# Attention maxima in pairs of 512 keys, with the turned maxima kept in the score ring

## The reference

```python
v = (values @ Wv.T).reshape(N, -1, H, Dh)
k = (keys @ Wk.T).reshape(N, -1, H, Dh)
q = (query @ Wq.T).reshape(N, -1, H, Dh)
energy = jnp.einsum('nqhd,nkhd->nhqk', q, k)
attn = jax.nn.softmax(energy / jnp.sqrt(jnp.float32(EMBED_DIM)), axis=3)
out = jnp.einsum('nhql,nlhd->nqhd', attn, v).reshape(N, -1, H * Dh)
return out @ Wo.T + bo
```

## Time and profile before

| what | value |
|---|---|
| timed runs, median of 3 | 3645.14 us (3643.07 to 3645.18) |
| the profiled execution, its own time | 3645.8 us |
| its span, first to last instruction | 3644.0 us |
| granted TensorE clock, mean of the span | 0.966 |
| busy: TensorE matmul, VectorE, ScalarE, GpSimd | 3391.9, 2494.9, 1520.4, 226.7 us |
| attention units, first scores to last values | 316.0 to 1509.4 us |

### The profile page before, as it was taken

The page is one execution under the profiler, slowest core; times in us unless marked ns, Lnnn a source line. Parts: engine busy times, 40 slices in busy tenths (PEclk is TensorE's granted clock), DMA queues, the critical chain, the costliest instruction groups (busy, mean ns, idle before and its releaser), DMA issues. The chain is left out here.

```text
span 3644.0 us, 63094 instructions
## 1 busy us (share of the span) xinstructions
PE 3391.9 (93%) x21900; PEld 2020.3 (55%) x21900; DVE 2494.9 (68%) x5808; ACT 1520.4 (42%) x2718; POOL 226.7 (6%) x251
## 2 busy tenths in 40 slices
PE   8979999999999999769977999977999999999999
PEld 5643222222222222258854545546989898989888
DVE  4538888888888888250013444438888888888885
ACT  4534777777777777412211222212222222222221
POOL 0021100000000000030000000000000000000000
PEclk9987999999999999879988999998999999999999
DMA  5687646465554642141120212112000000000000
GB/s 213 240 253 94 82 64 84 67 78 73 74 78 67 85 63 33 52 174 38 37 86 30 90 59 71 60 55 103 9 13 10 12 10 12 10 12 10 12 10 9
DMA packets 144167, 239.79 MB, mean 66 GB/s; under 512 B 22808, under 2 KB 100224, under 8 KB 143488
## 3 DMA queue, kind: packets, MB, share of 16 engines
q1 hardware_dynamic: 134768, 220.67, 28.6%
q0 software_dynamic: 4608, 12.59, 1.1%
q10 hardware_dynamic: 4624, 4.46, 0.4%
HBM read 170.38 MB, written 66.86 MB: 65 GB/s over the span
## 5 line engine op out<-in xcount | busy, mean ns | idle before, releaser
L656 DVE TENSOR_REDUCE at_pmax<-at_psm 128x2 f32<-128x800 f32 (+1 forms) x1024 | 968.1, 986 | 115.8 <-PE at_psm L504 94.0
L597 ACT ACTIVATE ring<-at_pss 128x512 f32<-128x512 f32 (+1 forms) x1664 | 865.2, 600 | 302.6 <-PE at_pss L518 298.3
L518 PE MATMUL at_pss<-at_qs,at_ks 99*128 99x512 bf16 (+1 forms) x1664 | 506.8, 386 | 8.0 <-ACT ring L597 6.5
L1659 PE MATMUL mt_psd<-mt_xl,mt_key_in 128*128 128x128 f32 x4096 | 491.1, 278 | 2.3 <-DMA mt_key_out<-m_out 2.3
L1659 PEld LDWEIGHTS mt_psd<-mt_xl,mt_key_in 128*128 128x128 f32 x4096 | 469.7, 193 | 3.7 <-DMA mt_key_out<-m_out 2.4
L1685 PE MATMUL mt_psu<-mt_key_out,mt_g 128*128 128x256 f32 x2048 | 447.4, 379 | 1.3 <-DVE mt_g L1895 1.3
L526 PE MATMUL at_pso<-ring,at_vw 128*32 128x512 f32 (+1 forms) x3328 | 444.1, 606 | 0.0
L1685 PEld LDWEIGHTS mt_psu<-mt_key_out,mt_g 128*128 128x128 f32 x2048 | 386.7, 190 | 52.6 <-DVE mt_g L1895 1.4
L502 PE MATMUL at_psm<-at_ks,at_qs 64*128 64x400 bf16 (+1 forms) x1024 | 340.1, 347 | 42.6 <-DVE at_pmax L656 18.9
L502 PEld LDWEIGHTS at_psm<-at_ks,at_qs 64*128 64x128 bf16 x1024 | 88.8, 93 | 467.0 <-DVE at_pmax L656 312.7
L504 PE MATMUL at_psm<-at_kh,at_qh 64*128 64x400 bf16 (+1 forms) x1024 | 339.8, 347 | 0.0
(11 more groups left out here) (218 smaller groups left out, 3781.7 us busy)
## 6 DMA issues: line engine op xcount, KB each, us to landing
at_ks<-k_dram SPq DMA_DIRECT2D x192, 200.1 KB, 6.7
k_dram<-pj_kp SPq DMA_DIRECT2D x24, 800.5 KB, 5.5
v_dram<-pj_v SPq DMA_DIRECT2D x8, 1664.0 KB, 9.1
at_vd<-v_dram SPq DMA_DIRECT2D x32, 416.0 KB, 10.7
pj_ctx<-ctxT SPq DMA_DIRECT2D x8, 1601.0 KB, 11.7
at_kh<-k_dram SPq DMA_DIRECT2D x128, 100.1 KB, 5.6
aw_ctxT<-ctxT SPq DMA_DIRECT2D x8, 1601.0 KB, 7.2
at_qs<-q_dram SPq DMA_DIRECT2D x192, 64.0 KB, 7.0
```

Of the source, the lines that this page charges most:

```text
L518: nc.tensor.matmul(ps_s[0:r, (NST * g + n) % SBANKS, :], ks[:, g, j, kt * P:kt * P + r], qs[:, g, j, :], start=True, stop=True).then_inc(s ...
L597: nc.scalar.activation(pr[0:r, (NST * g + n) % PRING, :], ps_s[0:r, (NST * g + n) % SBANKS, :], ACT.Exp, scale=SCALE).then_inc(expd, 1)
L656: nc.vector.tensor_reduce(pmax[:, 2 * p:2 * p + 2, q, c:c + 1], ps_m[:, n % MBANKS, :, 0:MSPANS[c][1]], AX.X, ALU.max).then_inc(m_red, 1)
L1659: ins = nc.tensor.matmul(ps_d[:, j % 2, y * P:y * P + P], key_in[:, k, j * YB + y, :], xl[:, s, k, :], start=k == 0, stop=k == KC - 1)
```

## The change

The spans become three of 512 keys, the width of one buffer half, and a rest of 65 keys. A unit has 24 jobs with one pair each, and two jobs (one for each head pair) that hold the rest for all four query tiles: eight matmuls of 65 columns, reduced by one instruction with eight results. So there are 26 jobs, two in each step, all between the third and the fourth score; `THREE` and `plan` go.

The turned maxima are written to a slot of the score ring, behind the first score of step 10, and every later score of the ring moves on by one slot. ScalarE copies the turned block to SBUF (`turned_out`) behind the exponential of that score. The split is made by GpSimd out of that copy. The pieces of `invert` move to jobs 14, 16 and 18. The loops of VectorE and GpSimd over the units are written out. The DMA of the bias goes ahead of the first `rows_out`, and before the first unit the six key products that are left stand together.

```diff
...
-    MSPANS = [(a, n) for a, n in spans(KEYS - 1, 400)]
-    MSPANS = [(0, 401)] + [(a + 1, n) for a, n in MSPANS[1:]]
-    NM = len(MSPANS)
-    max_jobs = [(p, q, c) for p in range(HG // 2) for q in range(QT) for c in range(NM)]
+    MSPAN = 512
+    NFULL, REST = KEYS // MSPAN, KEYS % MSPAN
+    NM = NFULL + 1
+    max_jobs = [(p, q, c) for p in range(HG // 2) for q in range(QT) for c in range(NFULL)]
+    max_jobs += [(p, None, NFULL) for p in range(HG // 2)]
...
-    INVERT_IN, INVERT_AT = 3, (17, 18, 22)
+    INVERT_IN, INVERT_AT = 3, (14, 16, 18)
...
-    THREE = (2, 3, 5, 7, 8, 11, 13)
...
-    def pairs_at(kt):
-        return {BETWEEN: 1 if kt == TURN_AT else 2, "values": int(kt in THREE)}
-    EARLY = sum(sum(pairs_at(kt).values()) for kt in range(TURN_AT, KT + 1))
-    order = iter([*range(EARLY, NJ), *range(EARLY)])
-    plan = {kt: {place: [next(order) for _ in range(n)] for place, n in pairs_at(kt).items()} for kt in range(1, KT + 1)}
-    assert next(order, None) is None
+    PER_STEP = NJ // KT
+    assert NJ == PER_STEP * KT and QT * REST <= MSPAN
+    EARLY = PER_STEP * (KT + 1 - TURN_AT)
+    TURN_BEHIND = TURN_AT * HG
+    def jobs_at(kt):
+        first = (kt - 1) * PER_STEP + EARLY
+        return [n % NJ for n in range(first, first + PER_STEP)]
+    def score_slot(u, n):
+        return (1 + u * (NST + 1) + n + (n > TURN_BEHIND)) % SBANKS
+    def turn_slot(u):
+        return ((u - 1) * (NST + 1) + TURN_BEHIND + 2) % SBANKS if u else 0
     with Stage(nc, "at") as st:
...
+        mfull, mrest, mpart = st.sb("mfull", [HG * QT, P]), st.sb("mrest", [HG * QT, P]), st.sb("mpart", [HG * QT, 3, P], BF16)
...
+        bo_in, biased, m_copied, own_split = sem("at_bo"), sem("at_biased"), sem("at_max_copied"), sem("at_own_split")
...
-        turned_at = ps_m[0:HG * QT, 1, 0, 0:P]
+        def turned_at(u):
+            return ps_s[0:HG * QT, turn_slot(u), 0:P]
...
                 for g in range(G - 1):
...
+                sp.dma_start(bo[:, :], t["bo_in"]).then_inc(bo_in, 16)
...
-                sp.dma_start(bo[:, :], t["bo_in"]).then_inc(bo_in, 16)
                 with sp.Fori(0, B - 1) as b:
                     for g in range(G):
...
                 def max_product(b, g, u, n):
...
-                    a, w = MSPANS[c]
+                    a = c * MSPAN
                     if n == 0:
...
-                    if n == 1:
-                        pe.wait_ge(m_parts, u + 1)
...
-                    nc.tensor.matmul(ps_m[:, n % MBANKS, 0, 0:w], qs[0:MAX_ROWS, g, 2 * p, q * P:q * P + P],
-                                     ks[0:MAX_ROWS, g, 2 * p, a:a + w], start=True, stop=True)
-                    nc.tensor.matmul(ps_m[:, n % MBANKS, 1, 0:w], qh[MAX_ROWS:2 * MAX_ROWS, g, p, q * P:q * P + P],
-                                     kh[MAX_ROWS:2 * MAX_ROWS, g, p, a:a + w], start=True, stop=True).then_inc(m_mm, 1)
+                    for q, to, w in [(x, x * REST, REST) for x in range(QT)] if q is None else [(q, 0, MSPAN)]:
+                        nc.tensor.matmul(ps_m[:, n % MBANKS, 0, to:to + w], qs[0:MAX_ROWS, g, 2 * p, q * P:q * P + P],
+                                         ks[0:MAX_ROWS, g, 2 * p, a:a + w], start=True, stop=True)
+                        ins = nc.tensor.matmul(ps_m[:, n % MBANKS, 1, to:to + w],
+                                               qh[MAX_ROWS:2 * MAX_ROWS, g, p, q * P:q * P + P],
+                                               kh[MAX_ROWS:2 * MAX_ROWS, g, p, a:a + w], start=True, stop=True)
+                    ins.then_inc(m_mm, 1)
                 def turn_max(u):
...
-                    nc.tensor.transpose(turned_at, nmax[:, :], t["ident"][:, :]).then_inc(m_turned, 1)
+                    if u:
+                        pe.wait_ge(expd, (u - 1) * NST + TURN_BEHIND + 2)
+                    nc.tensor.transpose(turned_at(u), nmax[:, :], t["ident"][:, :]).then_inc(m_turned, 1)
                 def scores(u, g, n):
...
-                    pe.wait_ge(expd, u * NST + n + 1 + (SBANKS - 1 if g == n == 0 else 0))
-                    nc.tensor.matmul(ps_s[0:r, (NST * g + n) % SBANKS, :], ks[:, g, j, kt * P:kt * P + r], qs[:, g, j, :],
+                    behind = n - TURN_BEHIND
+                    if behind == 3:
+                        pe.wait_ge(m_copied, min(u + 2, UNITS))
+                    elif u == 0 and n == 2:
+                        pe.wait_ge(m_copied, 1)
+                    else:
+                        pe.wait_ge(expd, u * NST + n + 1 + (behind in (1, 2)))
+                    nc.tensor.matmul(ps_s[0:r, score_slot(u, n), :], ks[:, g, j, kt * P:kt * P + r], qs[:, g, j, :],
...
                 def values(u, g, n):
...
-                    def maxima(place, kt):
+                    def maxima(kt):
...
                         if ahead is not None:
-                            for n in plan[kt].get(place, ()):
+                            for n in jobs_at(kt):
...
                     for kt in range(1, KT + 1):
...
                         for j in range(HG):
-                            maxima(j, kt)
+                            if j == BETWEEN:
+                                maxima(kt)
                             if kt < KT:
...
                             elif nxt is not None:
...
-                        if nxt is not None and kt == TURN_AT:
-                            turn_max(u + 1)
+                            if kt == TURN_AT and j == 0 and nxt is not None:
+                                turn_max(u + 1)
                         if kt == 1:
...
                         for j in range(HG):
...
-                        maxima("values", kt)
...
                 for n in range(NJ):
...
-                max_product(0, 1, 1, 0)
-                turn_max(0)
-                for n in range(1, EARLY):
+                for n in range(NJ, MH * len(halves)):
+                    key_product(n)
+                for n in range(MBANKS):
...
+                turn_max(0)
+                for n in range(MBANKS, EARLY):
+                    max_product(0, 1, 1, n)
...
                 for b in range(B):
                     for g in range(G):
...
-                        nc.scalar.activation(pr[0:r, (NST * g + n) % PRING, :], ps_s[0:r, (NST * g + n) % SBANKS, :],
+                        nc.scalar.activation(pr[0:r, (NST * g + n) % PRING, :], ps_s[0:r, score_slot(u, n), :],
...
+                        if n == TURN_BEHIND and u + 1 < UNITS:
+                            turned_out(u + 1)
                 def sums_out(u):
...
+                def turned_out(u):
+                    act.wait_ge(m_parts, u + 1)
+                    act.wait_ge(m_turned, u + 1)
+                    nc.scalar.activation(mfull[:, :], turned_at(u), ACT.Copy).then_inc(m_copied, 1)
+                turned_out(0)
...
                 for u in range(UNITS):
...
             def _(dve):
...
-                dve.sem_inc(m_parts, 1)
                 for n, name in enumerate("qkv"):
...
                     else:
...
-                def split(u, me):
-                    dve.wait_ge(m_turned, u + 1)
-                    dve.wait_ge(m_in, u * 48 + 1)
-                    me.then(nc.vector.tensor_copy(mpart[:, 0, :], turned_at))
-                    me.then(nc.vector.tensor_tensor(mrest[:, 0, :], turned_at, mpart[:, 0, :], ALU.subtract))
-                    me.then(nc.vector.tensor_copy(mpart[:, 1, :], mrest[:, 0, :]))
-                    nc.vector.tensor_tensor(mpart[:, 2, :], mrest[:, 0, :], mpart[:, 1, :], ALU.subtract).then_inc(m_parts, 1)
-                def maxima(u, me, before=None, behind=None):
+                def maxima(u, me=None, behind=None):
                     for n, (p, q, c) in enumerate(max_jobs):
                         if behind is not None and n in INVERT_AT:
...
-                        if n == 0 and before is not None:
-                            split(before, me)
+                        if n == 0:
+                            dve.wait_ge(m_all, u)
...
-                        nc.vector.tensor_reduce(pmax[:, 2 * p:2 * p + 2, q, c:c + 1], ps_m[:, n % MBANKS, :, 0:MSPANS[c][1]],
-                                                AX.X, ALU.max).then_inc(m_red, 1)
+                        heads, found = pmax[:, 2 * p:2 * p + 2, :, :], ps_m[:, n % MBANKS, :, :]
+                        if q is None:
+                            heads, found = heads[:, :, :, c], found[:, :, 0:QT * REST].rearrange("p j (q n) -> p j q n", n=REST)
+                        else:
+                            heads = heads[:, :, q, c:c + 1]
+                        nc.vector.tensor_reduce(heads, found, AX.X, ALU.max).then_inc(m_red, 1)
...
+                    dve.wait_ge(m_turned, u)
...
-                OWN_MAX, OWN = 3, 3 + 2
-                maxima(0, Own(dve, own))
-                maxima(1, Own(dve, own), 0)
-                with dve.Fori(1, UNITS - 1) as u:
-                    me = Own(dve, own, u, OWN)
-                    me.n = OWN_MAX - OWN
```

(25 more changed lines are left out.)

2 lines of the change are left out of this document (removed).

## The result

The changed kernel takes 3581.41 us (median of 4, 3577.34 to 3586.94) against 3644.63 (median of 4) run beside it: ratio 0.9828, 95% interval 0.9811 to 0.9845. Forecast was 3587, range 3567 to 3618. The profiled execution of the change took 3586.94 us, its span 3585.3, 58.7 less than the span before.

A forecast was written before the change was run, and what follows sets the result against it. TensorE was taken as the bound, with VectorE making it stumble: 2.7 us of waits in a 37.38 us unit. Gains of 56 in the units and 3 ahead of them, off 3645.8, gave 3587, range 3567 to 3618.

The forecast's parts named there:

- Ordinary step: A unit's steps with two pairs of 512 keys: 2.61 us each on TensorE, 2.52 plus 0.09.
- rival 2: VectorE stays the brake: reduces over two full banks 1.25 apart hold second pairs; unit 37.2, time 3637; chance 0.08.
- Rest pairs: Step 9's two pairs, each eight 65-column matmuls in four rounds: 0.04 us a round, 0.16 a pair, step 2.48.
- Rivals 1 and 4: Step 9: 1, weight loads not hidden, 3604, chance 0.12; 4, rest pairs in series, 3717, chance 0.03.
- Step 10: The step with the turn: its third score waits for the first exponential; 3.3 us instead of 2.61, +0.7.
- Steps 5 and 7: Inversion pieces on VectorE hold the second pair of step 5 by 0.47 us and step 7 by 0.28.
- Accumulator: At a unit's start ScalarE's accumulator copy pushes the first score's exponential, so the fourth score waits: +0.13 us.
- Units' gain: All attention units together: 1.83 us gained a unit, 31 x 1.69 + 30 x 0.13 = 56 us.
- Ahead of the units: Before the first unit: turn some 2 us earlier, first scores about 3 us earlier, bounds 0 and 5.
- Split: Splitting moved from VectorE to GpSimd: the parts land before step 13 needs them, with 1.4 us of slack.
- Rival 3: The parts land late: GpSimd's operations at 1.28 each, 1.7 late in step 13; unit 37.2, time 3638; chance 0.04.
- Rival 5: More gain: inversions and ring wait cost nothing; unit 34.5, time 3555; chance 0.04.

The follow-up runs named there:

- the bias late: The changed kernel with the bias DMA and its addition back behind the first two units' rows; 3585.69 us, ratio 0.9832.
- twelve more copies: The changed kernel with twelve more copies of 16x128 in GpSimd's split; 3661.85 us.
- two reorderings: The changed kernel with step 10's two pairs before its second score and inversion pieces ahead of jobs 0, 1, 2 of the next round; 3546.93 us, ratio 0.9736.

## Why the prediction was right, and where not

The mechanism held: TensorE bound, stumbling over banks that VectorE frees late; 26 jobs in even steps end that. What it had wrong in the account of the kernel before is where the waits were: it put them at VectorE's pause and at the inversion pieces, which held 0.40 and 0.49 a unit, while 1.7 of the 2.7 stood in the seven stretches with a third pair. Its sum did not hang on that, since it was built up from the new order. By its own steps:

- *Ordinary step* 2.61: measured 2.61 to 2.64. *Reduces* 1.22 long, 1.13 apart: 1.220 and 1.14. The fit without slack held, so rival 2 (VectorE stays the brake) falls; the pieces at odd jobs show how thin the margin is, some 25 us for the same work one job later.
- *Rest pairs*: a round 0.04, measured 0.031 to 0.035; a pair 0.16, and what stands between the pairs is a wait of about 0.09 for VectorE that the tally had left out. Rivals 1 and 4 fall. The rule of the Trainium skill (TensorE: Matmul & The Clock Gate, LDWEIGHTS (loading the stationary operand)), by which a load of 128 columns takes 107 ns, is near the recorded 0.093, but it is no spacing: rounds with fresh weights start 0.031 apart. As a spacing it would have made a unit an estimated 0.5 longer than it is.
- *Step 10* 3.3: 3.32, the third score at 1.14. *Steps 5 and 7*: +0.47 and +0.28 forecast, 0.38 and 0.17 measured, since the pieces cost 0.74 and 0.63, not 0.82 and 0.63, and the pair catches up a little sooner. *Accumulator* +0.13: step 1 took 2.67, so +0.06. Against these stand 0.05 more in step 9, 0.09 in step 11 and ordinary steps that are 0.01 above 2.61 in the mean. The unit came out at 35.36, 0.19 below 35.55.
- *Units' gain* 56 us: 61.7 from the first scores to the end of attention. This term was 6 too small, the size of 0.19 over 31 units.
- *Ahead of the units* -3: in the profiled execution +4.6. This is the step that failed, in its sign. It has three parts. The turn was at 306.59, 1.0 earlier than the 307.63 of the kernel before, and not some 2. From the turn to the first row's issue it took 2.61 by ScalarE and GpSimd where VectorE had needed 1.60, so the rows were issued at 309.20, no earlier than the 309.23 before; the prediction had no term for this longer way here. And their landing had no term here either; the rows on record had 1.7 to 3.3 us, and they took 6.3 to 10.0 in a queue that had not run dry. TensorE itself was ready at 313.9, 2.1 earlier than before, so that much of the term was right, and the rows took it back and 4.6 more. In the second profile of the same kernel they took up to 5.4 and the first scores came 1.0 earlier than before; with the bias late, 2.6 earlier. The bounds of 0 and 5 earlier needed a lower end below nothing. The two misses, -6 and +7.6, cancelled: that the total of 3587 met the profiled 3586.94 is luck, better than its parts. By the medians the gain is 63, not 59.
- *Split*: a slack of 1.4 us was forecast, and 2.5 measured. The four GpSimd operations take 1.63, not 2.0, the copy 0.25, not 0.4. Rival 3 was real further out (twelve more copies), and dearer than its sum, since the clock fell with it.
- The lower end of the range adds up to 3568 (14, 2 and 3 below 3587), not 3567; it bears on nothing.
- What the prediction did not see is that the parts of the change are not additive, and that the ring wait of step 10 (0.6) and most of what the pieces cost (0.35) are avoidable by order alone. Rival 5's 34.5 a unit, for which it saw nothing, was passed by two reorderings: 34.33.
